# Two-layer graph network, layer two: the four receiver masks of a group made by one wide VectorE operation

## What is computed

```
h   = relu(layernorm(x))
ef  = relu(edge_attr @ We1 + be1) @ We2 + be2
ef  = ef * sigmoid(edge_weight * Wt + bt)
msg = relu(concat(h[src], ef) @ Wn1 + bn1) @ Wn2 + bn2
x   = x + segment_sum(msg, dst) + h
```

## Time and profile before

| | |
|---|---|
| Time, median of 3 executions | 3255.13 us (3254.9 to 3264.79) |
| The profiled execution's own time | 3247.73 us |
| Its span, first to last instruction | 3245.9 us |
| Mean granted TensorE clock | 0.68 |
| Busy: TensorE, VectorE, ScalarE, GpSimd | 1748.3, 1541.0, 604.1, 1554.8 us |
| Layer two's edge work, by its first masks' start, to the end | 1771.8 to 3245.9 us |

### The profile page before, as it was taken

How to read it: one execution, slowest core, us unless ns; L and a number is a source line. 1 busy time by engine, 2 the same in 40 slices (tenths; PEclk the granted TensorE clock), 3 DMA queues, 4 the chain that set the end, 5 groups by cost and what they waited for, 6 DMA issues and landing times.

```text
span 3245.9 us, 44492 instructions
## 1 busy us (share of the span) xinstructions
PE 1748.3 (54%) x8785; PEld 1199.9 (37%) x8785; DVE 1541.0 (47%) x5471; ACT 604.1 (19%) x1276; POOL 1554.8 (48%) x1650
## 2 busy tenths in 40 slices
PE   2245443443433344253536775666666666766668
PEld 2233332332322233232334443444444444444446
DVE  2255545454433444354554554444444444444447
ACT  2320000000000000000235332222222222222223
POOL 5515555554544545453063554544445455444451
PEclk9665555555555555555667887877777788777788
DMA  4201111111111111111032333323323333333323
GB/s 119 60 16 42 42 43 40 44 40 36 40 33 33 43 31 43 35 38 29 2 110 75 85 98 94 95 77 92 93 77 95 93 83 92 93 94 95 83 86 110
DMA packets 114385, 213.29 MB, mean 66 GB/s; under 512 B 36899, under 2 KB 78030, under 8 KB 104127
## 3 DMA queue, kind: packets, MB, share of 16 engines
q0 software_dynamic: 51424, 106.19, 13.3%
q1 hardware_dynamic: 54930, 101.96, 10.9%
q10 hardware_dynamic: 7756, 2.31, 0.4%
HBM read 197.43 MB, written 12.88 MB: 65 GB/s over the span
## 4 chain that ended last, share of the span: by engine, by line
SPq 56%; issue 34%; PE 3%; another core or an unknown queue 2%; DVE 2%; ACT 1%; DMA 0%; POOL 0%; ACTq 0%; DVEq 0%; POOLq 0%
SPq L419 24%; SPq L1320 22%; SPq L109 8%; SPq L1316 1%; SPq L1315 1%; PE pair L1424 0%; PE pair L1418 0%; DVE acc L670 0%; PE bank L1433 0%; PE bank L1444 0%; ACT feat L1475 0%; PE bank L1453 0%; DVE moments L1547 0%; ACT ef L1475 0%
## 5 line engine op out<-in xcount | busy, mean ns | idle before, releaser
L1367 POOL DMA_INDIRECT acc<-table,index x806 | 766.0, 950 | 756.8 <-DVE pre L1612 461.5
L472 POOL DMA_INDIRECT rows<-table,index x753 | 716.4, 951 | 737.1 <-PE pair L973 386.0
L1418 PE MATMUL pair<-ea,we 64*128 64x512 f32 x416 | 271.6, 737 | 305.4 <-DMA ea<-in_ea_t 295.7
L665 DVE TENSOR_SCALAR onehot<-iota_row,dst_rel 128x128 f32<-128x128 f32 x808 | 238.4, 296 | 373.3 <-remote 310.2
L1627 DVE TENSOR_TENSOR acc<-acc,bank 128x128 f32 x832 | 239.0, 287 | 300.1 <-remote 122.6
L973 PE MATMUL pair<-onehot,rows 128*128 128x128 f32 x1560 | 380.7, 418 | 0.0
L973 PEld LDWEIGHTS pair<-onehot,rows 128*128 128x128 f32 x1560 | 327.6, 309 | 64.0 <-issue 59.0
L670 DVE TENSOR_TENSOR acc<-acc,pair 128x256 f32 x832 | 349.0, 420 | 4.3 <-issue 1.3
L1433 PEld LDWEIGHTS bank<-wn1b,ef 128*128 128x128 f32 x1664 | 273.8, 236 | 165.1 <-issue 116.5
L1424 PE MATMUL pair<-hidden,we 128*128 128x512 f32 x416 | 281.1, 763 | 78.3 <-ACT hidden L1503 68.2
L1593 DVE SCALAR_TENSOR_TENSOR ef<-pair,be,gate 128x512 f32<-128x512 f32 x208 | 155.3, 746 | 331.1 <-PE pair L1424 234.8
(11 more groups left out here) (186 smaller groups left out, 1539.2 us busy)
## 6 DMA issues: line engine op xcount, KB each, us to landing
ts<-in_ts SPq DMA_DIRECT2D x52, 1024.0 KB
rows_x<-table SPq DMA_DIRECT2D x2176, 0.5 KB
rows_y<-table SPq DMA_DIRECT2D x2048, 0.5 KB
ea<-in_ea_t SPq DMA_DIRECT2D x52, 512.0 KB
moments<-table ACTq DMA_DIRECT2D x1536, 0.5 KB
rows_z<-table ACTq DMA_DIRECT2D x1024, 0.5 KB
acc<-table,index POOLq DMA_INDIRECT x806
rows<-table,index POOLq DMA_INDIRECT x753
```

The source lines that it names most:

```text
L472: gp.indirect_dma_start(rows0[:, n % (RING * TG), :], None, table1, bass.IndirectOffsetOnAxis(index[:, n:n + 1], 0)).then_inc(half_in[g % ...
L1367: gp.indirect_dma_start(rows[:, g % RG1, t, :], None, table, bass.IndirectOffsetOnAxis(index[:, n:n + 1], 0)).then_inc(gathered[g % RG1], 16)
L1418: pe.matmul(bank[g % 2][:, :], we1[:, :], ea[:, g // HALF % 2, edges(g)], start=True, stop=True).then_inc(h1, 1)
```

## The change

The loop over the four tiles of a group, one TENSOR_SCALAR (compare with a scalar of each partition) of 128x128 each, becomes one TENSOR_TENSOR of 128x512. Its first input is `iota_row` (the numbers 0 to 127) repeated for the four tiles, its second are four columns of `dst_rel`, each repeated 128 times along the row. The signal `oh1` rises once per group instead of four times, and `aggregate` waits accordingly. The first layer's masks (line 665) stay as they are.

```diff
                 def aggregate(g):
                     pe.wait_ge(r2, g + 1)
-                    pe.wait_ge(oh1, (g + 1) * TG)
+                    pe.wait_ge(oh1, g + 1)
...
                 def masks(g):
                     if g >= 2:
                         dve.wait_ge(agg1, g - 1)
-                    for t in range(TG):
-                        q = g * TG + t
-                        dve.tensor_scalar(onehot[:, g % 2, t, :], iota_row[:, :], dst_rel[:, q:q + 1], None, ALU.is_equal).then_inc(oh1, 1)
+                    dve.tensor_tensor(onehot[:, g % 2], iota_row[:, :].unsqueeze(1).broadcast_to([P, TG, P]),
+                                      dst_rel[:, g * TG:(g + 1) * TG].unsqueeze(2).broadcast_to([P, TG, P]), ALU.is_equal).then_inc(oh1, 1)
```

## The result

| | median | lowest to highest |
|---|---|---|
| before, 4 executions | 3255.02 us | 3248.12 to 3264.79 |
| changed, 4 executions | 3219.15 us | 3215.02 to 3228.6 |

The ratio is 0.9892, 95% interval 0.9858 to 0.9925: the change made the kernel faster by about 36 us, 1.1%. I had forecast no change, 3253.4 us, and a range down to 3245. The profiled execution took 3228.6 us, the longest of the four; before, the profiled one took 3247.73 us.

The account below looks back on a forecast made before the run. SP's queue of row fetches in layer two was taken as the bound. Drain 0.4 us plus gathers 1.3 us made 1.7 us less, from the median 3255.13 to 3253.4 us; range 3245 to 3263 us.

Parts of the forecast that it names:

- The bound: Layer two: SP's queue of 2048 row fetches, 1428 us, holds back the compute engines and is never held back by them.
- Part 1: VectorE's masks: one wide operation takes 0.60 us where four narrow ones took 0.78, saving 37 us of VectorE time.
- Parts 2 and 3: The 37 us of VectorE time are nearly all covered by SP's stream; the drain behind SP's last fetch saves 0.4 us.
- Part 4: Gathers beside masks: the narrow masks' lengthening of gathers goes, worth at most 2.7 us to SP; half taken, 1.3 us.
- the excess: Mean over median gather time, 806 x 6 ns = 4.8 us, taken as all that narrow masks cost GpSimd.
- one undisturbed pair: A TENSOR_TENSOR at 3153.47 inside a gather begun at 3153.41, both keeping their usual 0.28 and 0.94 us.
- 0.56 of each microsecond in which gathers run: SP's loss beside gathers, from fetches 0.72 us apart with gathers and 0.32 without: 4.8 us are worth at most 2.7.
- B: Wide mask and gathers shut each other out: 125 us more gathering, 70 us felt by SP, 3325 us; chance 0.06.
- A: VectorE paces layer two after all, its stalls reaching SP: time falls by 37 us, to 3218; chance 0.04.
- C: Phase between SP and GpSimd moves past 0.3% either way, to about 3243 or 3267 us; chance 0.06.
- phase shifts of 5 us: Shorter bursts shift gathers against SP's register and big loads: 10 us, half of that expected at most, in either direction.
- signs of being wrong: SP's stream over 10 us shorter or longer, gathers over 1 us beside wide masks, or time moving while the stream does not.

Follow-up runs that it names:

- the first experiment: Kernel before, with each of layer two's four narrow masks made by TENSOR_TENSOR of 128x128 in place of TENSOR_SCALAR: ratio 0.9984.
- 69 pauses: Kernel before, plus a GpSimd memset of 128x512 after the second gather of every third group: ratio 0.9876 where SP is slowed, 1.0117 on a quick chip.
- 208 pauses: Kernel before, plus a GpSimd memset of 128x512 once in every group: ratios 1.0385, 1.0373 and 1.0382, all on quick chips.
- The two halves: The change with its wide mask split into two of 128x256, a signal each; against the kernel before, ratios 1.0036 and 1.0041 on quick chips.
- wide mask and 208 pauses: The change plus a GpSimd memset pause once in every group, against the kernel before: ratio 1.0451 on a quick chip.

## Why the prediction was wrong

**The bound.** Right as far as it went: SP's queue is the chain, it waits for VectorE's `pre` but once (14.2 us, after), and the profile after has the same chain. The runs with added and removed VectorE work confirm it. I had both of SP's speeds in hand, but did not ask whether the slow one is the same at every place of a burst; it is not.

**Part 1, the masks.** Right: 684 ns against the 0.69 expected, and in the timeline above the next instruction starts 0.60 us behind. The cycle table of the Trainium skill ("VectorE: DVE Perf Modes", section on the errata) had the wide one right too, 0.59 us. The narrow ones gain nothing from being TENSOR_SCALAR: 287 ns each so, 285 ns as TENSOR_TENSOR in the first experiment.

**Parts 2 and 3, cover and drain.** Right in that the 37 us of VectorE time are covered. TensorE's wait for `ea`, which was to stay or grow, fell from 295.7 to 276.8 us while SP's stream got shorter. The drain's 0.4 us is too little to be seen; the end behind the stream got 11 us longer in the one profile, and I have no cause for that.

**Part 4 failed, twice.** I wrote that the wide mask leaves gathers alone, "So I take the excess to go", from one undisturbed pair. In that pair the gather began first, by 0.06 us, and the VectorE operation lasts 0.28 us. The order matters, as counted above, and so does the length: four operations of 128x128 in a row leave the longest gather at 1073 ns, while one of 128x512 makes it 1471. The row was of the right kind, and of the wrong order and length. The excess was not all the masks' either: of the 75 gathers before that last over 975 ns, 39 began under the operation of line 1635, and without masks the mean is still 948 ns. Then I priced a longer gather as a loss to SP, "0.56 of each microsecond in which gathers run". The sign is wrong for holds. The gathers got 18 us longer here, 22 us in the repeat of the change (806 x 27 ns) and were put off by 29 us with the 69 pauses, and the median times fell by 36, 44 and 41 us; the profiled streams took 42, 29 and 49 us less than the 1427.7 of the kernel before, the last two on another occasion than that one. I had taken two speeds, with and without gathers, for a law of time. SP's loss grows as gathers follow each other without a break, and a delay of 0.4 us early in a burst makes the burst longer but gives SP more than that back. In place of 1.3 us, what the gathers and the mask do to each other was worth about 36.

**The rivals.** B had the mechanism, wide mask and gather shutting each other out, with the price of the wrong sign here: it was to make 3325 us. Where GpSimd is the bound, on the quick chips, B is what happens, at 19 us in place of my 125, since only some 65 masks in 208 meet a gather at the wrong moment and hold it by 0.1 to 0.5 us. A had the right time, 3218 us, by luck, for a reason that the runs rule out. C, a larger shift of gathers against SP, went to about 3243 on the fast side. The range, 3245 to 3263, was drawn from phase shifts of 5 us; a change of 1.1% through the spacing of gathers was not among my cases at all. Of the signs of being wrong that I named, two came up: the stream shorter by over 10 us, and gathers of over 1 us beside wide masks.

**What stays open.** That gathers slow SP, and that pauses in them relieve it, is shown. How, inside the queues and the DMA engines, is not, nor why the quick chips show none of it. Nor do I know whether 208 pauses would help more than 69. The counts above say that a pause helps only early in a burst; no run placed pauses by that. The two halves, meant to show a smaller dose, were measured on quick chips only. No version beat both kernels everywhere: 69 pauses equal the change where SP is slowed (0.9876 and 0.9879) and cost 1.2% where it is not.

## What to carry to other kernels

When a queue that issues small transfers is the chain, ask what sets its pace before calling every change elsewhere covered: a change that touches neither the queue nor anything it waits for can still space out the traffic beside it. A wide VectorE operation with both inputs in SBUF delays a GpSimd gather that starts under it, here by up to 0.5 us; whether that costs or pays depends on who paces the stage. Before taking an undisturbed pair of instructions for proof that two kinds leave each other alone, look which of them began first, and how long they last. And a gain that comes this way belongs to a chip's condition: measure it on more than one chip before keeping it, since here the same edit gave 0.989 and 1.008.

## What the runs showed of the hardware that I had not expected

- One program, two kinds of chip: 3255 to 3333 us on three occasions, 2135 us on three others, which were two chips. On the quick ones, 2048 row fetches of SP took 906 us with gathers running; on the others 1379 to 1479 us with them and 904.7 us without.
- A TENSOR_TENSOR of 128x512 with both inputs in SBUF, begun before a gather, held it up to 1474 ns (wide mask and 208 pauses) where the median is 947; of 128x256, up to 1211 ns; of 128x128, up to 1073 ns, which is hardly more than with narrow TENSOR_SCALAR masks (1029 before, 1065 with 208 pauses). Begun 0.15 us or more behind the gather, it did not hold it at all. The Trainium skill, "SBUF — State Buffer", section on who interferes with whom, has a two-input operation contend with a GpSimd instruction that reads SBUF: the trace agrees if a gather, which reads its row numbers there, is one.
- Pausing the engine that gathers made the program faster: 29 us of pauses, 41 us less time (3265.44 to 3224.49).
- What gathers cost SP's queue builds up over a burst of them: before the change 2.1 fetches start between the first two gathers, 1.0 from the fifth on, in the same 1.25 us.
